# Preparing the second block's weights in the attention's last slots: transposed inputs, low parts on GpSimd, first products moved

## The chip, the cores and the metric

One core of a Trainium2 chip runs the whole kernel in one launch. The metric is device microseconds of one execution; lower is better. The engines are TensorE (PE, with its weight loads PEld), VectorE (DVE), ScalarE (ACT), GpSimd (POOL) and SyncE (SP), which issues nearly all DMAs. Each runs its own instruction list in order and waits on semaphores.

## The reference

Two decoder-like blocks on x of 16x64x512, with a context of the same shape. Only what the border between them touches is spelled out:

```python
# block 0: attention (32 query heads, 8 key/value heads of 128), then a quantised gated feed-forward
x = x + tanh(g_xattn[0]) * attention0(layernorm(x), ctx, mask, wq, wk, wv, wo)
x = x + tanh(g_ffn[0])   * quant_ffn(layernorm(x), Wg, Wu, Wd)
# block 1: q = Wq c + bq, k = Wk c + bk over 64 channels of the context, attention over the 512 positions
q = einsum('dc,bct->btd', Wq, init) + bq
k = einsum('dc,bct->bdt', Wk, init) + bk
out = softmax(q k) @ (einsum('oc,bct->bto', Wv, x) + bv)
# block 1: a base product and a low-rank part of 4 chosen experts out of 16, weighed by a router
y = einsum('bth,oh->bto', x, W_base) + b_base
z = einsum('bth,erh->bter', x, lora_A[active])
y += einsum('bteo,bte->bto', einsum('bter,eor->bteo', z, lora_B[active]) * 2, softmax(log(prior) + router(x)))
```

Products in full float32 are made of "hi" and "lo" parts: a ScalarE copy rounds a tensor to the hi part, a subtraction on another engine gives the lo part, and TensorE adds hi x hi, hi x lo and lo x hi.

## The kernel before

There are two programs, one after the other, without a barrier between them. The first, `attention_block`, does block 0's attention in 32 slots numbered U (0 to 31): 8 groups of key/value heads, two query-head pairs each, two halves of the tokens each. A slot of TensorE (`slot` under `@block.tensor`) holds in this order: the four output tiles of the unit before, `output(U - 1)` (six matmuls each, lines 521, 522, 526); four transposes of the probabilities (line 615); the scores of unit U + 1 (`score_unit`, line 503); the product with the values (line 628, "av"); then up to three projection items (lines 81 to 83). Slots 30 and 31 have no items left. What sets the order is the order written by hand in each engine's list, plus the semaphores.

The output tiles alternate between two PSUM banks, so tile k must wait until VectorE has added tile k - 2 into `x_res`: `output_tile` waits on `s_acc`, which `accumulate` (VectorE, line 927) raises, and which starts at 2:

```python
pe.wait_ge(s_acc, UT * U + tl + 1)
```

The other engines per slot: ScalarE copies the transposed probabilities (line 748), copies av to `oT_hi` (823), takes the exponential of the next unit (700), and evacuates projections (695, 696). VectorE adds four tiles (927), does the softmax of the next unit in `soft_first` (scale and mask 907, maximum 912, subtraction 914), makes `oT_lo` (1104), and sums the exponentials (921, 923). GpSimd multiplies by the inverse sum (1188), and rotates (1174, 1180) and splits (1151) the slot's projections.

The second program, `last_programs` (feed-forward of block 0 and block 1 interleaved by hand in `tensor`, `scalar`, `vector`, `gpsimd`, `sync`), needs prepared weights and the first tile of the context. This is the border, and it is made in slots 30 and 31 and just behind them:

- `load_block1` and `load_base` (SyncE) load the small weights and W_base. `lora_B` comes with 4 DMAs in runs of 8 floats.
- TensorE: `qkv_T` (533) transposes Wq, Wk, Wv; `base_T(0..3)` (545) transposes W_base, four 128x128 blocks each; `b_T` (561) transposes lora_B; `low_T` (552, 553, 556) picks the active experts' rows with selection matrices; `low_b_select` (567) does the same for lora_B; `first_qk` (576, 577) makes q and k of the first context tile. `qkv_T` and `base_T(0)` end slot 30; `base_T(1)` and `(2)` stand ahead of av in slot 31; `base_T(3)`, `b_T` behind it; then output tile 0 of unit 31, `first_qk`, `low_T((0, 1))`, tile 1, `x_transpose(0)` (1515), tile 2, `gate_mm(0, 0)` (1525) and so on, with `low_T((2, 3))` much later, behind `gate_mm(0, 2)`.
- ScalarE: `qkv_weights` (769, 772), `base_high_part` (776), `bT_copy` (780), `first_split_hi` (796), `first_hi_qk` (800), `low_part` (785 to 788).
- VectorE: `selection_of_experts` (from 1016), `selection_matrices` (to 1034), `gated_rows` (1061), `router_offset` (1055, 1057), `qk_w_low_part` (1040), `base_low_part` (1045), `first_lo_qk` (1050). In slot 31 also the statistics of tiles 0 to 3 (1072), and behind it `first_front` (1133), which quantises the first tile for the feed-forward; ScalarE ends that with line 1423.
- GpSimd: two iotas and two memsets at the head of slot 30 (1230 to 1233), raising `s_zero`; the low part of the first context tile (1246), the inverse deviation (1250), and four memsets (1255) for which SyncE waits before it starts its list of the second program.

```python
if U == 2 * NPAIR - 2:
    pool.iota(M.rank_i[:, :], pattern=[[1, RANK]], base=0, channel_multiplier=0).then_inc(s_zero, 1)
    pool.iota(M.part_i[:, :], pattern=[[0, 1]], base=0, channel_multiplier=1).then_inc(s_zero, 1)
    pool.memset(f32(M.qk_w_lo[:, :]), 0.0).then_inc(s_zero, 1)
    pool.memset(M.v_w[:, :], 0.0).then_inc(s_zero, 1)
```

## Time and profile before

| | us |
|---|---|
| three runs | 797.85, 799.20, 799.59; median 799.20 |
| the profiled execution | 797.15, of which its span is 795.3 |
| TensorE busy | 783.9 (99%), granted clock 1.00 |
| VectorE busy | 542.8 (68%) |
| ScalarE busy | 437.7 (55%) |
| GpSimd busy | 496.0 (62%) |
| TensorE busy between 563 and 582 | 18.0 of 19 |
| VectorE busy between 563 and 604 | 39.1 of 41 |

Times in the rows are microseconds from the span's start. A matmul's end is modelled and overlaps the next one's start, so on TensorE the distance from one start to the next is the cost of a piece of work. The attention's last slot but one (U = 30) starts on TensorE at 553.4, slot 31 at 563.6, and the second program's first gate product at 581.3.

### The profile page before, as it was taken

To read this page: it belongs to the slowest core of one execution; us is meant where nothing else is said; L and a number is where in the kernel's file an instruction comes from. 1 tells how busy PE (TensorE), PEld (TensorE's weight loads), DVE (VectorE), ACT (ScalarE), POOL (GpSimd) and SP (SyncE) were. 2 spreads that over 40 slices of the span, in tenths; PEclk is the share of its full clock that TensorE was granted. 3 is DMA by queue.
4 is the path that set the end of the run, shared out by engine and by line. 5 is a ranking of instruction groups with operands and counts; after the bars stand their busy time and mean duration, and the time that the engine had idled before them with its cause. 6 is when DMAs were issued, how large, how long until landed. Compare 5 with 4: busy or idle time off the path is not lost.

```text
span 795.3 us, 13637 instructions
## 1 busy us (share of the span) xinstructions
PE 783.9 (99%) x4977; PEld 643.0 (81%) x4994; DVE 542.8 (68%) x1043; ACT 437.7 (55%) x825; POOL 496.0 (62%) x429
## 2 busy tenths in 40 slices
PE   8999999999999999999999999999999999999998
PEld 8888888888888888788888888888765777777776
DVE  5867776566677545565665455465899997998874
ACT  4754445444444434443445343334579898888773
POOL 1697567645656764566666456645457885877753
PEclk9999999999999999999999999999999999999999
DMA  9411623523543131963213220167273413223101
GB/s 305 136 68 39 167 79 80 133 73 88 144 88 90 40 102 38 56 128 80 87 40 95 51 53 27 33 73 254 91 193 100 107 47 81 74 48 81 47 15 40
DMA packets 89986, 71.02 MB, mean 89 GB/s; under 512 B 53648, under 2 KB 69232, under 8 KB 89536
## 3 DMA queue, kind: packets, MB, share of 16 engines
q1 hardware_dynamic: 89248, 69.82, 35.8%
q8 instruction: 40, 0.66, 0.4%
q10 hardware_dynamic: 672, 0.33, 0.1%
q14 instruction: 26, 0.21, 0.1%
HBM read 49.04 MB, written 6.34 MB: 70 GB/s over the span
## 4 chain that ended last, share of the span: by engine, by line
PE 94%; DVE 3%; ACT 1%; DMA 1%; issue 0%; POOL 0%; SPq 0%; DVEq 0%
PE bank L81 12%; PE bank L83 12%; PE bank L82 12%; PE bank L526 7%; PE bank L521 7%; PE bank L522 7%; PE bank L503 7%; PE bank L628 4%; PE bank L1602 4%; PE bank L1588 3%; PE bank L1554 2%; PE bank L1525 2%; PE bank L1533 2%; PE bank L1578 2%; PE bank L615 2%; PE bank L1579 2%
## 5 line engine op out<-in xcount | busy, mean ns | idle before, releaser
L927 DVE SCALAR_TENSOR_TENSOR x_res<-bank,gate,x_res 128x512 f32<-128x512 f32 x128 | 95.4, 747 | 74.6 <-PE bank L526 74.2
L1188 POOL TENSOR_TENSOR prob<-prob,row_inv 128x512 f32<-128x512 f32 x32 | 33.5, 1046 | 168.5 <-DVE row_inv L923 168.5
L1174 POOL TENSOR_TENSOR rope_swap<-rope_swap,trig 128x512 f32<-128x512 f32 x80 | 103.6, 1296 | 34.2 <-ACT rope_swap L696 33.9
L695 ACT COPY rope_swap<-bank 64x512 f32<-64x512 f32 x80 | 46.7, 584 | 111.2 <-DVE rope_cos L898 108.7
L898 DVE TENSOR_TENSOR rope_cos<-bank,trig 128x512 f32<-128x512 f32 x80 | 54.2, 678 | 76.8 <-PE bank L83 74.4
L521 PE MATMUL bank<-wo_hi,oT_hi 128*128 128x512 f32 x256 | 101.8, 398 | 2.1 <-DVE x_res L927 1.5
L81 PE MATMUL bank<-xnT_hi,wq_hi 128*128 128x512 f32 x256 | 103.1, 403 | 0.0
L83 PE MATMUL bank<-xnT_hi,wq_lo 128*128 128x512 f32 x256 | 101.6, 397 | 0.0
L82 PE MATMUL bank<-xnT_lo,wq_hi 128*128 128x512 f32 x256 | 101.2, 396 | 0.0
L522 PE MATMUL bank<-wo_lo,oT_hi 128*128 128x512 f32 x256 | 100.9, 394 | 0.0
L1180 POOL TENSOR_TENSOR q_rope<-rope_cos,rope_swap 128x512 f32<-128x512 f32 x64 | 84.2, 1316 | 5.0
L526 PE MATMUL bank<-wo_hi,oT_lo 128*128 128x512 f32 x256 | 80.6, 396 | 0.3 <-DVE oT_lo L1104 0.2
L2946 POOL TENSOR_TENSOR b_e<-b_e,b_inv 128x512 f32<-128x512 f32 x64 | 68.3, 1081 | 18.9 <-DVE b_inv L2139 18.4
L748 ACT COPY probT<-bank 128x512 f32<-128x512 f32 x32 | 18.7, 585 | 101.9 <-PE bank L615 101.9
L823 ACT CAST oT_hi<-bank 128x512 fp32r<-128x512 f32 x64 | 34.4, 589 | 68.9 <-PE bank L628 68.9
L503 PE MATMUL bank<-k_rope,q_rope 128*128 128x64 f32 x512 | 61.0, 272 | 0.0
L521 PEld LDWEIGHTS bank<-wo_hi,oT_hi 128*128 128x128 f32 x256 | 48.2, 188 | 15.4 <-DVE x_res L927 2.5
L503 PEld LDWEIGHTS bank<-k_rope,q_rope 128*128 128x128 f32 x512 | 59.7, 192 | 0.5
L81 PEld LDWEIGHTS bank<-xnT_hi,wq_hi 128*128 128x128 f32 x256 | 48.1, 188 | 12.9
L526 PEld LDWEIGHTS bank<-wo_hi,oT_lo 128*128 128x128 f32 x256 | 48.0, 188 | 12.2 <-DVE oT_lo L1104 1.2
L83 PEld LDWEIGHTS bank<-xnT_hi,wq_lo 128*128 128x128 f32 x256 | 48.1, 188 | 11.3
L82 PEld LDWEIGHTS bank<-xnT_lo,wq_hi 128*128 128x128 f32 x256 | 48.1, 188 | 10.9
(257 smaller groups left out, 1943.9 us busy)
## 6 DMA issues: line engine op xcount, KB each, us to landing
wq_raw<-in_L_xattn_wq SPq DMA_DIRECT2D x16, 512.0 KB, 3.9
wo_raw<-in_L_xattn_wo SPq DMA_DIRECT2D x16, 512.0 KB, 3.9
xn<-in_L_ffn_Wd SPq DMA_DIRECT2D x16, 256.0 KB, 3.2
b_ctx<-in_ctx SPq DMA_DIRECT2D x32, 128.0 KB, 2.7
b_k_twice<-b_qk_hi SPq DMA_DIRECT2D x32, 128.0 KB, 2.4
w_T_dram<-w_out SPq DMA_DIRECT2D x28, 128.0 KB, 3.4
w_T<-w_T_dram SPq DMA_DIRECT2D x2, 1376.0 KB, 17.7
xn<-in_L_ffn_Wg SPq DMA_DIRECT2D x10, 256.0 KB, 3.3
```

What stands on the lines that cost most here:

```text
L81: pe.matmul(out, a_hi, b_hi, start=first, stop=False)
L82: pe.matmul(out, a_hi, b_lo, start=False, stop=False)
L83: return pe.matmul(out, a_lo, b_hi, start=False, stop=last)
L503: mm = pe.matmul(score[:, n * S:(n + 1) * S], q_rope[jp][:, b], k_rope[:, b * S:(b + 1) * S], start=True, stop=True)
L521: pe.matmul(out, oT_hi[:, tl, h], wo_hi[jp][:, h, :], start=(h == 0), stop=False)
L522: pe.matmul(out, oT_hi[:, tl, h], wo_lo[jp][:, h, :], start=False, stop=False)
L526: mm = pe.matmul(out, oT_lo[:, tl, h], wo_hi[jp][:, h, :], start=False, stop=(h == 1))
L898: dve.tensor_tensor(out=rope_cos[:, rp, :].rearrange("p (b s) -> p b s", s=S), in0=proj[stream % 2][:, :].rearrange("p (b s) -> p b s", s= ...
L927: dve.scalar_tensor_tensor(out=K.x[:, t, :], in0=wo_ps[t % 2][:, :], scalar=K.gate[:, 0:1], in1=K.x[:, t, :], op0=ALU.mult, op1=ALU.add).t ...
L1174: pool.tensor_tensor(out=sw, in0=sw, in1=sin_b, op=ALU.mult).then_inc(s_rope, 1)
L1180: pool.tensor_tensor(out=dst, in0=rope_cos[:, rp, :].rearrange("p (b s) -> p b s", s=S), in1=sw, op=ALU.add).then_inc(s_rope, 1)
L2946: pool.tensor_tensor(out=e[m % 4][:, :], in0=e[m % 4][:, :], in1=inv_total[:, n:n + 1].to_broadcast([P, D]), op=ALU.mult).then_inc(s_w, 1)
```

## The change

W_base, Wq and Wk, Wv, and lora_B are laid out on the host and loaded as they are used. That removes `qkv_T`, `base_T`, `b_T` and `bT_copy`. W_base's low parts are subtracted by GpSimd from SBUF. Several steps get another place. The memset of `v_w` is gone (its zeros are in the loaded tensor).

TensorE (the two waits that come first are in `low_T`: the one for 9 ahead of chunks 0 and 1, the one for 11 ahead of its last matmul; in the slot, the first pair of edits lies between the probability transposes and av, the second behind av; `x_transpose(0)` now waits for `s_w_low`):

```diff
+                pe.wait_ge(s_sel, 9)
+                pe.wait_ge(s_soft, 5 * (2 * NPAIR - 1) + 1)
...
+                pe.wait_ge(s_sel, 11)
...
             def first_qk(par):
                 if par == 0:
-                    pe.wait_ge(s_w_qkv, 4)
+                    pe.wait_ge(s_w_qkv, 1)
                     pe.wait_ge(s_w_qkv_lo, 1)
-                    pe.wait_ge(s_oT_lo, 2 * 2 * NPAIR)
+                    pe.wait_ge(s_proj_read, len(ALL))
...
                 if U == 2 * NPAIR - 1:
-                    base_T(1)
-                    base_T(2)
+                    low_T((0, 1))
...
                 if U == 2 * NPAIR - 2:
-                    qkv_T()
-                    base_T(0)
+                    first_qk(0)
+                    first_qk(1)
+                if U == 2 * NPAIR - 1:
+                    low_T((2, 3))
             run_slots(slot)
-            base_T(3)
-            b_T()
...
-            first.qk(0)
-            first.qk(1)
-            first.low_T((0, 1))
             first.output(2 * NPAIR - 1, 1)
             x_transpose(0)
...
             gate_mm(0, 2)
-            first.low_T((2, 3))
```

ScalarE (the first edit of the slot lies behind the copy of the transposed probabilities, the second behind `oT_hi`, the last two at the slot's end):

```diff
             def qkv_weights():
-                act.wait_ge(s_w_ps, W_QKV)
-                act.wait_ge(s_zero, 4)
...
+                act.wait_ge(R1.s_in, 16 * R1.n_loads)
+                act.wait_ge(s_zero, 3)
+                act.copy(M.qk_w_hi[:, :], R1.qk[:, :]).then_inc(s_w_qkv, 1)
+                act.copy(M.v_w[:, :], R1.v[:, :]).then_inc(s_w_qkv, 1)
...
                         probT_copy(U)
-                    if U == 2 * NPAIR - 1:
+                    if U == 2 * NPAIR - 2:
+                        first_split_hi(1)
                         base_high_part(1)
+                        base_high_part(2)
                     act.wait_ge(s_av, U + 1)
...
+                    if U == 2 * NPAIR - 2:
+                        first_hi_qk(0)
+                        first_hi_qk(1)
                     if U < 2 * NPAIR - 1:
                         exp_unit(U + 1)
...
+                    if U == 2 * NPAIR - 3:
+                        qkv_weights()
+                        first_split_hi(0)
+                        base_high_part(0)
                     if U == 2 * NPAIR - 2:
-                        qkv_weights()
-                        base_high_part(0)
-                        first_split_hi(0)
-                        first_split_hi(1)
+                        base_high_part(3)
                         prior_logarithm()
             run_groups(body)
-            base_high_part(2)
-            base_high_part(3)
-            bT_copy()
+            low_part()
```

VectorE (the first edit stands in the loop over the four tiles, behind `accumulate`):

```diff
                 for k in range(UT):
+                    if U == 2 * NPAIR - 2:
+                        (qk_w_low_part, selection_of_experts, selection_matrices, gated_rows)[k]()
                 if U == 2 * NPAIR - 2:
-                    selection_of_experts()
-                    selection_matrices()
-                if U < 2 * NPAIR - 1:
+                    soft_scale(U + 1)
+                    output_low(U)
+                    soft_shift(U + 1)
+                elif U < 2 * NPAIR - 1:
                     soft_first(U + 1)
+                    output_low(U)
                 else:
                     statistics_end()
-                    base_low_part(1)
-                    gated_rows()
                     router_offset()
+                    output_low(U)
                 if U < 2 * NPAIR - 1:
                     soft_sum(U + 1)
-                if U == 2 * NPAIR - 2:
-                    qk_w_low_part()
-                    base_low_part(0)
...
-            base_low_part(2)
...
-            first.base_low(3)
```

GpSimd:

```diff
                         pool.memset(f32(M.qk_w_lo[:, :]), 0.0).then_inc(s_zero, 1)
-                        pool.memset(M.v_w[:, :], 0.0).then_inc(s_zero, 1)
+                        first_split_lo(0)
+                        first_split_lo(1)
+                        pool.wait_ge(M.s_ctx_lo[1], 1)
+                        base_low_part(0)
+                        base_low_part(1)
                     if U < 2 * NPAIR - 1:
                         normalise(U + 1)
...
             run_groups(body)
-            pool.wait_ge(s_prob, 2 * NPAIR)
-            for par in range(2):
...
+            base_low_part(2)
+            base_low_part(3)
             pool.wait_ge(s_x_stat, 2 * UT + 1)
```

`first_split_lo` is the removed loop's body, `base_low_part` VectorE's old one with `R1.base` in SBUF in place of a PSUM bank. `qk_w_low_part` now waits for `s_w_qkv` at 1 (it was 4) and reads `R1.qk` in SBUF. `low_T` writes to the score bank, `first_qk` to the projection banks. SyncE issues one DMA for lora_B (4 before), and two for Wq, Wk and Wv (3 before).

## Rows read from the trace of the kernel before

**Rows 1.** The page: busy time of the engines.

```profile
PE 783.9 (99%) x4977; PEld 643.0 (81%) x4994; DVE 542.8 (68%) x1043; ACT 437.7 (55%) x825; POOL 496.0 (62%) x429
```

**Rows 2.** Windows: length, busy PE, PEld, DVE, ACT, POOL, granted clock, DMA share, GB/s.

```profile
563.00:573.00 10.00, 9.33 (x58) 6.99 (x56) 9.72 (x22) 8.08 (x17) 3.98 (x4) 1.00 0.01 2
...
592.00:604.00 12.00, 10.81 (x61) 6.65 (x60) 11.90 (x24) 10.74 (x24) 11.66 (x10) 1.00 0.41 110
```

**Rows 3.** The chain that ended last, 557 to 582: start, us, what.

```profile
557.60 0.23 PE bank L521
...
562.48 1.08 ACT oT_hi L823 x2
...
563.59 1.29 DVE oT_lo L1104 x2
564.88 0.60 DVE row_max L921
...
566.45 0.67 DVE x_res L927
...
575.94 0.24 PE bank L576
...
581.31 0.81 PE bank L1525 x3
```

**Rows 4.** Timeline of VectorE: start, us, line, [idle before].

```profile
554.86 0.75 DVE L927 SCALAR_TENSOR_TENSOR x_res<-bank,gate,x_res 128x512 f32<-128x512 f32 x1 [0.70 <-PE bank L526]
...
559.71 0.16 DVE L1016 CAST l_act_f<-l_act_i 128x4 f32<-128x4 int32 x1
...
562.11 0.69 DVE L912 TENSOR_REDUCE row_max<-prob 128x8 f32<-128x512 f32 x1
562.83 0.69 DVE L914 TENSOR_TENSOR prob<-prob,row_max 128x512 f32<-128x512 f32 x1
...
582.26 0.75 DVE L2070 SCALAR_TENSOR_TENSOR f_gate<-bank,f_x_scale,w_row 128x512 f32<-128x512 f32 x1 [0.55 <-PE bank L1525]
```

**Rows 5.** Timeline of GpSimd around the head of slot 30.

```profile
558.00 1.29 POOL L1180 TENSOR_TENSOR q_rope<-rope_cos,rope_swap 128x512 f32<-128x512 f32 x1
...
559.41 0.20 POOL L1232 MEMSET l_qk_lo<- 128x128 f32 x1
```

**Rows 6.** Timeline of ScalarE.

```profile
563.55 0.63 ACT L700 ACTIVATE prob<-prob 128x512 f32<-128x512 f32 x1
564.09 0.53 ACT L769 CAST l_qk_hi<-bank 64x128 fp32r<-64x128 f32 x2
...
578.32 0.72 ACT L1423 ACTIVATE f_xn<-f_xn,f_x_inv 128x512 f32<-128x512 f32 x1 [0.15 <-DVE f_x_inv L1417]
```

**Rows 7.** Timeline of TensorE: removed and moved pieces, and what follows each.

```profile
570.51 1.04 PE L545 MATMUL bank<-ident,l_raw_base 128*128 128x128 f32 x8
571.48 1.16 PE L628 MATMUL bank<-probT,v_nat 64*128 64x128 f32 x16
572.57 0.66 PE L545 MATMUL bank<-ident,l_raw_base 128*128 128x128 f32 x4
...
573.81 0.50 PE L521 MATMUL bank<-wo_hi,oT_hi 128*128 128x512 f32 x1
...
576.71 0.30 PE L552 MATMUL bank<-l_sel,l_raw_a 128*128 128x32 f32 x2
...
577.90 0.50 PE L521 MATMUL bank<-wo_hi,oT_hi 128*128 128x512 f32 x1
```

**Rows 8.** Waits of TensorE up to 560: total us, times, longest.

```profile
PE bank L521 <- DVE x_res L927: 1.5, 1, 1.5
```

**Rows 9.** Two timelines, VectorE and GpSimd, at the same moment.

```profile
587.83 0.68 DVE L2089 SCALAR_TENSOR_TENSOR f_h<-f_tanh,f_up 128x512 f32<-128x512 f32 x1
...
596.70 1.45 DVE L2089 SCALAR_TENSOR_TENSOR f_h<-f_tanh,f_up 128x352 f32<-128x352 f32 x1
...
596.50 1.27 POOL L2952 TENSOR_TENSOR b_ctx_split<-b_ctx,b_ctx_split 64x512 fp32r<-64x512 f32 x1
```

More of the change, by code:

```diff
@@ L554, in low_T @@
+                    pe.matmul(score[:, c * NLOW + NZ:(c + 1) * NLOW], R1.r[:, c * P:(c + 1) * P], M.sel_e[:, :], start=True, stop=True)
                 if cs[-1] < DC - 1:
                     return
-                pe.matmul(trans[:, HD:HD + E_ACT], M.spread[:, :], M.sel_e[:, :], start=True, stop=True).then_inc(s_w_lowT, 1)
-            def b_T():
-                pe.wait_ge(s_w_lo, 2)
-                for c in range(DC):
-                    mm = pe.transpose(proj[0][:, c * P:(c + 1) * P], R1.b[:, c, :], K.ident[:, :])
-                mm.then_inc(s_w_ps, 1)
+                pe.wait_ge(s_sel, 11)
@@ L633, in slot @@
                 if U == 2 * NPAIR - 2:
-                    qkv_T()
-                    base_T(0)
+                    first_qk(0)
+                    first_qk(1)
+                if U == 2 * NPAIR - 1:
+                    low_T((2, 3))
             run_slots(slot)
-            base_T(3)
-            b_T()
             output(2 * NPAIR - 1, (0,))
             first = Keep()
-            first.output, first.qk, first.low_T, first.low_b_select = output_tile, first_qk, low_T, low_b_select
+            first.output, first.low_b_select = output_tile, low_b_select
             tail.tensor(pe, first)
@@ L915, in soft_first, with output_low @@
                                   op=ALU.subtract).then_inc(s_soft, 1)
+            def soft_first(U):
+                soft_scale(U)
+                soft_shift(U)
+            def output_low(U):
+                dve.wait_ge(s_oT_hi, 2 * U + 2)
+                for par in range(2):
+                    dve.tensor_tensor(out=oT_lo[:, :, :, par, :],
+                                      in0=av[par][:, :].rearrange("p (t h q) -> p t h q", t=UT, h=2),
+                                      in1=f32(oT_hi[:, :, :, par, :]), op=ALU.subtract).then_inc(s_oT_lo, 1)
             def soft_sum(U):
@@ L1276, in block1_raw @@
     R, sb = Raw1(), area.take
-    R.qkv = [sb(f"l1_raw{i}", [S, S]) for i in range(3)]
+    R.qk, R.v = sb("l1_raw_qk", [P, P]), sb("l1_raw_v", [P, P])
     R.a = sb("l1_raw_a", [P, D])
-    R.b = sb("l1_raw_b", [P, DC, P])
+    R.b = sb("l1_raw_b", [P, D])
     R.r = sb("l1_raw_r", [E_ALL, D])
@@ L3264, in rope_table, with laid_out @@
     return np.ascontiguousarray(np.stack([cos, sin], axis=1).astype(np.float32))
+def laid_out(inputs):
+    a = {name: np.asarray(value) for name, value in inputs.items()}
+    base = a["L1_ffn_W_base"].T.reshape(DC, P, D).transpose(1, 0, 2)
+    qk = np.tile(np.concatenate([a["L1_xattn_Wq"].T, a["L1_xattn_Wk"].T], axis=1), (2, 1))
+    v_two = np.zeros((P, P), np.float32)
+    v_two[:S, :S] = v_two[S:, S:] = a["L1_xattn_Wv"].T
+    low_b = a["L1_ffn_lora_B"].transpose(0, 2, 1).reshape(P, D)
+    return [("base_T", base), ("qk_T", qk), ("v_T", v_two), ("lora_b_T", low_b),
+            ("rope_table", rope_table())]
 def kernel(**inputs):
@@ L3272 @@
     arrays, aps = {}, {}
-    for name, value in [*inputs.items(), ("rope_table", rope_table())]:
+    for name, value in [*inputs.items(), *laid_out(inputs)]:
         arrays["in_" + name] = v = np.ascontiguousarray(value)
```

124 lines of the change are left out of this document (40 added, 84 removed).

## The prediction

> **What bounds the kernel now.** The page comes first: TensorE is busy 99% of the span, its weight loads (81%) overlap it, and no other engine is over 68% [rows 1]. Over the whole kernel a microsecond taken from TensorE's list looks like a microsecond won. The windows around the border correct that. From 563 to 573 TensorE loses 0.7 us and VectorE is busy 9.72 of 10; from 592 to 604 TensorE loses 1.2 us and VectorE is busy 11.90 of 12 [rows 2]. So here VectorE sets the pace, and TensorE's transposes fill time in which it would partly wait. The chain says the same: it leaves TensorE at 562.46 (the end of av of unit 30), goes through ScalarE's `oT_hi`, VectorE's `oT_lo`, the sum of the exponentials and the addition of a tile, and stays on VectorE nearly until TensorE's 575.2 [rows 3]. The place ahead of it differs: at 557.60 TensorE is on the chain with the fourth tile of unit 29 [rows 3], and any wait put there is paid in full, because nothing ahead of 562.46 has slack on TensorE.
>
> **The change, first part: a new wait of VectorE in slot 30.** `qk_w_low_part` now stands behind the first of the four additions, and waits for ScalarE's copy, which waits for `s_zero` at 3, which GpSimd raises with the memset at the head of its slot 30. When is each there? The first addition starts at 554.86, and its result is there some 0.7 us later, at 555.55 [rows 4]. GpSimd works on its last rotation until 559.29 and ends the memset at 559.61 [rows 5]; the change takes nothing out of its list ahead of that. ScalarE's copy follows: two copies of 64x128 took 0.53, so one takes 0.27; the new one has 128 rows and reads SBUF; I bound it by 0.25 below and by the 0.63 of a 512-column ScalarE instruction above, and take 0.3, as the 64x128 copy is nearest [rows 6]: 559.92. The subtraction itself is of 64x128; 0.2 is an estimate from the 0.16 of a tiny instruction and the 0.69 of one of 512 columns [rows 4]. VectorE is free again at 560.12, having stood from 555.55 to 559.92.
>
> Queued behind it are the additions of tiles 1, 2, 3. TensorE's tile 3 needs the bank of tile 1, hence the second addition: 560.12 plus 0.67, as one such addition takes [rows 3], is 560.79, and TensorE starts the tile at 560.82. It did so at 557.60 [rows 3]. **That is +3.22 us**, and probabilities, scores and av follow in the same shape: av ends at 565.68, where it ended at 562.46. The selections that VectorE does in the same slot (they fill 559.71 to 562.11, together with the scaling of 0.7 [rows 4]), and its `gated_rows`, run while TensorE does the tile, transposes and scores; if they did not fit (say 1 us more), the scaling would be late, but `oT_lo` waits for av longer than that. I cost them at nothing. ScalarE's three copies ahead of `oT_hi` (0.6 each as the rows for 512 columns, [rows 6]) run before av ends; nothing again.
>
> **Second part: from av(30) to the third tile of unit 30.** Before: `oT_hi` and `oT_lo` end 2.42 behind av, and the addition of tile 0 ends at 567.12, that is 4.66 behind [rows 3]. After: VectorE does `oT_lo` first and then the maximum's reduction and the subtraction, 0.72 apart and 0.69 long [rows 4]; the exponential, 0.63, can only start then [rows 6]; then the sum, 0.60, the reciprocal, 0.2 with its start, and the addition, 0.67 [rows 3]. In all 2.42 + 0.72 + 0.69 + 0.63 + 0.60 + 0.2 + 0.67 = 5.93, with semaphore steps of 0.02 each about 6.0. TensorE has by then done `first_qk` and tiles 0 and 1 (at 4.6, as before) and waits for this addition: **+1.35 us**. What left VectorE here (`qk_w_low_part` and one base subtraction) is counted in the 4.66. What left TensorE (`qkv_T`, `base_T(0)`) lay where it waited for `oT_hi` anyway, and so does `first_qk` now.
>
> **Third part: slot 31 and the tiles of unit 31.** Eight transposes, 0.97, go from ahead of av(31), and `low_T((0, 1))`, 1.19, comes: +0.2. Behind av `base_T(3)` and `b_T`, 1.24, go, and `low_T((2, 3))`, 1.19 and one matmul more, comes; neither counts, as tile 0's last two matmuls wait for `oT_lo`, which follows from av. So tile 0 of unit 31 ends 1.35 + 0.2 = 1.55 later against av(30) than before: 13.48 then [rows 3], 15.0 now. Behind tile 0, `first_qk` (0.93) and `low_T((0, 1))` (1.19) go: −2.1 [rows 7]. But of this 2.1 only a part is won, as the next thing in TensorE's list waits for `x_transpose(0)`'s input. Before, tile 0 ended at 575.94, and ScalarE's last step of `first_front` at 579.04, 3.1 behind [rows 3, 6]; TensorE, with 3.5 us of work in between, didn't wait. Now there is one tile (1.4) in between, and TensorE waits 1.7. The quantised tile is there at 18.1, the transposes take 0.24, tile 2 takes 1.4 and a step 0.1, and the gate product starts at 19.85. Before it was 581.31, or 18.85 [rows 3]: **+1.0 us** in all, in place of the 1.55.
>
> **Fourth part: behind it.** VectorE waits 0.55 for the gate product at 582.26 [rows 4], so the base subtraction that leaves its list just ahead wins nothing. `low_T((2, 3))` leaves a stretch (589 to 591) of TensorE that ends in one bound by VectorE [rows 2]: worth nothing if VectorE never waits there, and 0.4 if the shorter of the two waits of [rows 2] (0.7 and 1.2) went by half; I take 0.2. GpSimd's and SyncE's lists start the second program some 1.2 us later against av(30), for GpSimd now has four base subtractions in between, some 1.3 each like its rotation [rows 5]; the duplicates of the first q and k then land just in time. The smaller loads on SyncE, far ahead, change nothing.
>
> One row is a warning for the upper end. A VectorE product of 352 columns took 1.45 us, where one of 512 took 0.68, while GpSimd ran a subtraction from 596.50 to 597.77 [rows 9]. The Trainium skill ("SBUF — State Buffer", Who interferes with whom) has it that a VectorE instruction with two SBUF inputs and a GpSimd one that reads SBUF exclude each other; this row agrees. Moving GpSimd's work deals such meetings anew; one costs up to 0.9 [rows 9].
>
> **Sum.** 3.22 + 1.0 − 0.2 = 4.0 us. The profiled execution took 797.15, so it would be 801.2; the median of three is 2 us above that execution, and on it the sum gives **803.2**.
>
> **The rivals.** *TensorE's list is all that counts (faster).* Removed are 0.97 and 1.24 [rows 7], and about 0.8 at the end of slot 30 (seven transposes, by the eight at 0.97), 3.0 in all: 796.2. It decides at one point: `s_w_qkv` must be raised before about 556.2, so that the second addition ends ahead of 557.6. It would need GpSimd to be 3.4 us earlier; GpSimd's records are rough, but ScalarE's and VectorE's around them are not. What speaks for it is the 99% [rows 1]. Chance 0.09.
>
> *The wait is there but the tail swallows it (no difference).* If the 0.7 and 1.2 us that TensorE loses in [rows 2], and its 3.0 us of transposes, could all be taken against the 3.2, little is left: 799.4. It needs the chain through `oT_lo` and the exponentials to be slack, which the chain shows it is not. Chance 0.10.
>
> *TensorE's clock falls over the new wait (still slower).* Its granted clock is 1.00 in every window of [rows 2], and over a wait of 1.5 us for the same addition [rows 8] nothing behind it took longer. A wait of 3.2 us no row shows. If the clock fell to the 1.2 GHz level, tile, transposes, scores and av behind it (from 557.60 to 562.46, 4.86 us) would at most double: up to 4.86 more, 808.1, and half of that 805.6. The Trainium skill ("TensorE: Matmul & The Clock Gate", What's actually happening) says that such a fall follows idleness. Chance 0.07.
>
> **The numbers.** Forecast 0.74, the three rivals 0.09, 0.10, 0.07. A run of this kernel can tell 0.2%, 1.6 us, from no change. The forecast's own range takes 0.2 off for `low_T`, 0.55 if VectorE's wait for the gate product [rows 4] is made good, adds 0.2 for `low_T`, 0.9 for one meeting, 0.3 for the copy, and the spread of the runs of before (1.4 below the median, 0.4 above): 801.0 to 805.0. To hold 8 in 10 it reaches to 800.0 below, towards the second rival, and to 805.6 above, past the lower price of the third. Faster 0.09, same 0.12, slower 0.79.
>
> **What would show it.** In the new profile VectorE's `qk_w_low_part` has an idle time of 4.4 us before it, released by ScalarE; TensorE waits some 3.2 us for the addition ahead of the last output tile of unit 29, and 1.3 ahead of the third of unit 30; `x_transpose(0)` waits over 1 us for ScalarE; the first gate product starts near 585.5. The forecast is wrong if VectorE's wait is under 1 us (then the first rival), or if the gate product is late but the wait of TensorE near 604 shrinks by as much.

## The result, and the profile after

The changed kernel takes 803.94 us, median of 10 runs (803.14 to 809.24), beside 798.34 for the kernel before on the same chip (10 runs, 797.11 to 802.37). The medians lie 5.6 us apart; the ratio is 1.008 with an interval of 1.0061 to 1.0098. The kernel is slower. The forecast was 803.2, with 800.0 to 805.6 as its range.

The page of the changed kernel, first the span and the engines (before: [rows 1]):

```profile
span 802.1 us, 13578 instructions
PE 782.9 (98%) x4954; PEld 641.2 (80%) x4971; DVE 542.7 (68%) x1039; ACT 437.0 (54%) x822; POOL 501.0 (62%) x432
```

The profiled execution took 803.9. TensorE is busy for 1.0 us less than before and needs 6.8 us more span, so what was added is mostly waiting. A part of the busy time is work at a lower clock, as shown below. The timeline of VectorE, around the head of slot 30, shows where:

```profile
555.23 0.75 DVE L911 SCALAR_TENSOR_TENSOR x_res<-bank,gate,x_res 128x512 f32<-128x512 f32 x1 [0.70 <-PE bank L523]
560.37 0.28 DVE L1024 TENSOR_TENSOR l_qk_lo<-l_raw_qk,l_qk_hi 64x128 fp32r<-64x128 f32 x1 [4.39 <-ACT l_qk_hi L739]
...
561.24 1.20 DVE L1000 CAST l_act_f<-l_act_i 128x4 f32<-128x4 int32 x1
...
564.94 1.31 DVE L1040 TENSOR_SCALAR l_base_row<-l_base_row,gate 128x512 f32<-128x512 f32 x1
566.17 1.24 DVE L1041 TENSOR_TENSOR l_bv<-l_bv,gate 128x1 f32<-128x1 f32 x1
```

The first addition (L911, line 927 of the kernel before) is followed by 4.39 us of nothing, released by ScalarE's copy. That copy, in ScalarE's timeline:

```profile
560.04 0.30 ACT L739 CAST l_qk_hi<-l_raw_qk 128x128 fp32r<-128x128 f32 x1 [4.30 <-POOL l_qk_lo L1214]
```

and what releases the copy, with what else GpSimd did, in GpSimd's timeline (compare [rows 5]):

```profile
559.75 0.20 POOL L1214 MEMSET l_qk_lo<- 128x128 f32 x1
561.14 1.27 POOL L1171 TENSOR_TENSOR b_ctx_split<-b_ctx,b_ctx_split 64x512 fp32r<-64x512 f32 x1 [1.19 <-ACT b_ctx_split L762]
564.70 1.27 POOL L1171 TENSOR_TENSOR b_ctx_split<-b_ctx,b_ctx_split 64x512 fp32r<-64x512 f32 x1 [2.29 <-ACT b_ctx_split L762]
566.04 2.60 POOL L1176 TENSOR_TENSOR l_base_lo<-l_raw_base,l_base_hi 128x512 fp32r<-128x512 f32 x2
```

It is a chain of three: memset, copy, subtraction, and behind the subtraction the second addition. In the kernel before, the tile that needs this addition started here:

```profile
557.44 0.40 PE L521 MATMUL bank<-wo_hi,oT_hi 128*128 128x512 f32 x1
```

TensorE's timeline of the changed kernel shows that tile's wait, and the waits that follow (L518 is line 521 of the kernel before):

```profile
561.37 0.50 PE L518 MATMUL bank<-wo_hi,oT_hi 128*128 128x512 f32 x1 [3.39 <-DVE x_res L911]
569.27 0.73 PE L523 MATMUL bank<-wo_hi,oT_lo 128*128 128x512 f32 x2 [0.59 <-DVE oT_lo L897]
572.83 0.50 PE L518 MATMUL bank<-wo_hi,oT_hi 128*128 128x512 f32 x1 [1.43 <-DVE x_res L911]
...
580.54 0.63 PE L519 MATMUL bank<-wo_lo,oT_hi 128*128 128x512 f32 x1
...
586.13 0.38 PE L1494 MATMUL bank<-ident_b,f_xn 128*128 128x128 bf16 x4 [1.56 <-ACT f_xn L1402]
588.03 0.38 PE L1504 MATMUL bank<-w_T,f_xqT 128*128 128x512 bf16 x1
610.95 0.22 PE L1525 MATMUL bank<-ident_b,f_h 128*128 128x128 bf16 x1 [0.84 <-ACT f_h L2522]
```

Forecast were waits of 3.2, 1.3 and 1.7; they are 3.39, 1.43 and 1.56. Not forecast are the 0.59, and the matmul of 0.63 us at 580.54, where such a one takes 0.39 elsewhere. The windows tell why (columns as in [rows 2]; the last but two is the granted clock):

```profile
578.00:580.00 2.00, 2.00 (x21) 1.76 (x17) 0.72 (x4) 1.07 (x2) 1.80 (x3) 1.00 0.00 0
580.00:582.00 2.00, 2.00 (x6) 1.61 (x6) 0.95 (x2) 0.73 (x3) 1.17 (x3) 0.50 0.00 0
582.00:584.00 2.00, 2.00 (x8) 1.57 (x7) 1.09 (x2) 0.00 (x0) 0.00 (x0) 0.65 0.57 146
```

At 580 the granted clock falls from 1.00 to 0.50 (from the 2.4 GHz level to the 1.2 GHz one), for some 3.4 us, in the middle of busy work and 7 us behind the last wait.

**How the runs below are compared.** Two profiles differ long before slot 30, in code that is the same: the first addition of slot 30 starts at 555.23 in one profile of the changed kernel and at 558.92 in the other. Near 340 us TensorE waits for an addition, 1.53 us before and 3.22 in the second profile of the changed kernel, and in that one the granted clock falls there too (as in those of `e3_gated_order` and `e7_memset`). So starts are counted from the first addition of slot 30. "The distance" is from there to the first gate product: 554.86 to 581.31 before, 26.45 us, and 26.34 in a second profile of the kernel before; 555.23 to 588.03 after, 32.80.

The columns give the starts on TensorE; the last one covers only the stretch from slot 30 to the gate product.

| kernel | probabilities of unit 30 | av(30) | probabilities of unit 31 | gate product | granted clock under 0.9 in |
|---|---|---|---|---|---|
| before | 3.98 | 6.41 | 15.21 | 26.45 | nowhere |
| before, second profile | 3.98 | 6.41 | 15.17 | 26.34 | nowhere |
| after | 7.65 | 9.91 | 20.49 | 32.80 | 580 to 584 |
| after, second profile (`a0`) | 8.33 | 11.51 | 21.61 | 32.79 | 566 to 570 |
| `e1_late` | 3.98 | 6.93 | 18.70 | 29.66 | nowhere |
| `e2_gated` | 8.88 | 11.29 | 21.39 | 32.35 | 562 to 566 |
| `e3_gated_order` | 8.43 | 11.50 | 19.90 | 32.32 | 562 to 568, 580 to 588 |
| `e4_all` | 3.98 | 6.92 | 17.90 | 30.00 | 578 to 582 |
| `e5_pool` | 3.98 | 6.91 | 16.90 | 29.32 | 576 to 580 |
| `b_wait` | 8.16 | 11.66 | 20.43 | 32.17 | 562 to 566 |
| `e7_memset` | 4.19 | 6.47 | 20.82 | 32.00 | 574 to 582 |
| `e8_memset_pool` | 4.19 | 6.47 | 17.98 | 30.08 | 570 to 574, 580 to 584 |
| `e6_own` | 3.97 | 6.44 | 14.86 | 25.69 | nowhere |

### The profile page after: what moved, and what is told of

It reads as the page before. It is cut to its first block, busy times and chain, and to the rows that moved or that the text cites. A ratio compares the mean times of both kernels' runs of the same rounds, so it can differ in the third digit from the quotient of the medians.

```text
span 802.1 us, 13578 instructions
## 1 busy us (share of the span) xinstructions
PE 782.9 (98%) x4954; PEld 641.2 (80%) x4971; DVE 542.7 (68%) x1039; ACT 437.0 (54%) x822; POOL 501.0 (62%) x432
## 4 chain that ended last, share of the span: by engine, by line
PE 92%; DVE 4%; POOL 2%; ACT 1%; issue 1%; DMA 1%; another core or an unknown queue 0%; SPq 0%; DVEq 0%; ACTq 0%
PE bank L81 12%; PE bank L83 11%; PE bank L82 11%; PE bank L523 7%; PE bank L518 7%; PE bank L519 7%; PE bank L500 7%; PE bank L600 4%; PE bank L1577 4%; PE bank L1563 3%; PE bank L1533 2%; PE bank L1504 2%; PE bank L1512 2%; PE bank L588 2%; PE bank L1555 2%; PE bank L1556 2%
## 5 line engine op out<-in xcount | busy, mean ns | idle before, releaser
L911 DVE SCALAR_TENSOR_TENSOR x_res<-bank,gate,x_res 128x512 f32<-128x512 f32 x128 | 95.4, 746 | 76.6 <-PE bank L523 74.9
L518 PE MATMUL bank<-wo_hi,oT_hi 128*128 128x512 f32 x256 | 102.5, 400 | 6.9 <-DVE x_res L911 5.0
L518 PEld LDWEIGHTS bank<-wo_hi,oT_hi 128*128 128x128 f32 x256 | 48.7, 190 | 21.1 <-DVE x_res L911 6.5
L519 PEld LDWEIGHTS bank<-wo_lo,oT_hi 128*128 128x128 f32 x256 | 48.6, 190 | 10.2
```

The costliest lines, as they stand in the source:

```text
L518: pe.matmul(out, oT_hi[:, tl, h], wo_hi[jp][:, h, :], start=(h == 0), stop=False)
L519: pe.matmul(out, oT_hi[:, tl, h], wo_lo[jp][:, h, :], start=False, stop=False)
L911: dve.scalar_tensor_tensor(out=K.x[:, t, :], in0=wo_ps[t % 2][:, :], scalar=K.gate[:, 0:1], in1=K.x[:, t, :], op0=ALU.mult, op1=ALU.add).t ...
```

## The experiments

The theory: VectorE's new wait in slot 30 costs 3.2 us, the order around `oT_lo` 1.35, and part of it comes back before the gate product. Rivals: only the rearranged weights matter, whatever the waits; or the clock makes the rest. The runs came in three batches, each with its own runs of the kernel before (medians 799.74, 797.97 and 802.12), so a median is compared inside its batch. The record also has a mean granted clock for each run, rounded to 0.001. It is 0.992 to 0.998 in the ten runs of the changed kernel. The kernel before has 1.000 in 13 of 28, 12 of 23 and 1 of 22 runs of the three batches: its clock falls too in some runs, and most often in the third.

**All four steps behind the fourth addition.**

```diff
-                    if U == 2 * NPAIR - 2:
-                        (qk_w_low_part, selection_of_experts, selection_matrices, gated_rows)[k]()
+                    if U == 2 * NPAIR - 2 and k == UT - 1:
+                        qk_w_low_part()
+                        selection_of_experts()
+                        selection_matrices()
+                        gated_rows()
```

> The changed kernel, with VectorE's four steps of slot 30 (qk_w_low_part, selections, gated_rows) behind its fourth addition in place of one behind each, so nothing of the additions queues behind the wait for s_w_qkv. My theory: the 3.4 us wait of TensorE ahead of the last tile of unit 29 goes, the 1.4 us one ahead of the third tile of unit 30 stays, and with less idling the granted clock stays at 1.00 near 580: about 4.5 us less than the changed kernel, some 799.5. Rival 1 (the wait costs but the clock falls all the same): about 3.2 us less. Rival 2 (the tail, not the wait, sets the time): under 1.5 us less.

Measured: 804.15 against 799.74, ratio 1.0053 (1.0028 to 1.0079); the distance is 29.66. The long wait is gone: the probabilities of unit 30 start 3.67 us earlier than in the first profile of the changed kernel. The distance is 3.14 shorter, and a part of that is the fall of the clock, which this one profile doesn't have. The median is not the 799.5 of the expectation: it is 4.4 above the kernel before, where the changed kernel stands 5.6 above it in its own batch, with intervals that overlap. So by time this run doesn't show what the wait costs. Eight of its ten runs have a mean clock of 0.998 or less. TensorE's waits in this kernel:

```profile
569.51 0.73 PE L523 MATMUL bank<-wo_hi,oT_lo 128*128 128x512 f32 x2 [1.58 <-DVE oT_lo L897]
573.07 0.50 PE L518 MATMUL bank<-wo_hi,oT_hi 128*128 128x512 f32 x1 [1.42 <-DVE x_res L911]
585.24 0.38 PE L1497 MATMUL bank<-ident_b,f_xn 128*128 128x128 bf16 x4 [1.85 <-ACT f_xn L1405]
```

A new one of 1.58 for `oT_lo` has come up: VectorE does the same small steps later, nearer to av, and several of them are stretched. Its timeline:

```profile
563.38 1.14 DVE L1008 TENSOR_SCALAR l_act_f<-l_act_neg 128x4 f32<-128x4 f32 x1
564.89 1.21 DVE L1018 TENSOR_SCALAR l_sel<-l_want,l_part_f 128x128 f32<-128x128 f32 x1
...
566.42 1.24 DVE L1041 TENSOR_TENSOR l_bv<-l_bv,gate 128x1 f32<-128x1 f32 x1
```

L1018 took 0.29 and L1041 0.15 in the changed kernel's second profile.

**The wait alone, in the kernel before.** Nothing of the change but two steps of the selections behind the first two additions.

```diff
-                if U == 2 * NPAIR - 2:
-                    selection_of_experts()
-                    selection_matrices()
+                    if U == 2 * NPAIR - 2 and k < 2:
+                        (selection_of_experts, selection_matrices)[k]()
```

> The kernel before, with selection_of_experts and selection_matrices behind the first and second addition of slot 30 in place of behind the fourth. The first waits for GpSimd's iotas at about 559.4. My theory: TensorE waits 3.2 to 3.5 us for the second addition, and the first gate product and all behind it come 3.2 to 3.5 us later, some 3.3 us more time. If the fall of the clock near 580 in the changed kernel was that wait's doing, it falls here too, and the distance to the gate product grows by up to 1.4 more. Rival: later slack takes most of the wait back, under 1.5 us.

Measured: 803.21 against 797.97, ratio 1.007 (1.0048 to 1.0092). VectorE waits behind its first addition, here for GpSimd's second iota:

```profile
559.39 0.20 DVE L1016 CAST l_act_f<-l_act_i 128x4 f32<-128x4 int32 x1 [3.93 <-POOL l_part_i L1230]
```

TensorE's timeline has the wait, with its restart, and the slow transposes and scores behind it:

```profile
561.00 0.50 PE L521 MATMUL bank<-wo_hi,oT_hi 128*128 128x512 f32 x1 [3.55 <-DVE x_res L927]
...
562.87 1.05 PE L615 MATMUL bank<-ident,prob 128*128 128x128 f32 x4
563.71 2.50 PE L503 MATMUL bank<-k_rope,q_rope 128*128 128x64 f32 x14
```

and its windows:

```profile
562.00:564.00 2.00, 2.00 (x9) 1.68 (x8) 0.89 (x2) 0.04 (x1) 0.00 (x0) 0.51 0.06 22
564.00:566.00 2.00, 2.00 (x14) 2.00 (x14) 0.00 (x0) 0.54 (x1) 0.00 (x0) 0.64 0.00 0
```

A wait at this one place makes 5.2 us by medians and 5.7 by the distance, nearly what the whole change makes, with all weights still transposed on TensorE. The rival of the rearranged weights falls. And behind the wait the clock comes down: from the last tile's start to av(30) there are 3.83 us before (557.44 to 561.27) and 5.37 here (561.00 to 566.37). So the wait costs 3.55 where it stands (the tile starts 3.71 later, counted from the first addition) and 1.5 more behind it. Another 0.5 is lost in the last stretch (11.74, before 11.24), where TensorE waits 0.69 for `oT_lo`.

The clocks of the single runs say the same. The four runs of `b_wait` have 0.997 to 0.998. The six runs of the kernel before with that clock have a median of 800.0, 3.2 us under `b_wait`; the twelve with 1.000 have 797.7. So of the 5.2 us some 3.2 are the wait and 2.0 go with the clock, an estimate from few runs.

**The changed kernel once more.**

> The changed kernel once more, on the chip of the next two. All theories: some 804 us, 5 to 6 above the kernel before on the same chip. It also shows where the granted clock falls in a second profile. If the fall belongs to the waits in slots 30 and 31, there is a window at 0.5 to 0.7 somewhere between 561 and 590, not necessarily at 580. If there is none and the time is the same, the clock is not part of the 5.6 us.

Measured: 809.22 against 802.12, ratio 1.0082 (1.0046 to 1.0118). Both kernels are slower on this chip, and both have lower mean clocks here (0.985 to 0.995 for the changed kernel). The difference of the medians, 7.1, has the widest interval of all. TensorE's timeline has the same wait:

```profile
565.07 0.50 PE L518 MATMUL bank<-wo_hi,oT_hi 128*128 128x512 f32 x1 [3.41 <-DVE x_res L911]
```

The windows have the fall directly behind the wait, and none at 580 or later:

```profile
566.00:568.00 2.00, 2.00 (x8) 1.60 (x7) 1.86 (x11) 0.00 (x0) 0.11 (x1) 0.50 0.37 144
568.00:570.00 2.00, 2.00 (x15) 2.00 (x14) 1.18 (x4) 1.65 (x4) 0.47 (x1) 0.71 0.00 0
...
580.00:582.00 2.00, 2.00 (x15) 1.72 (x14) 1.93 (x4) 0.58 (x1) 0.60 (x1) 1.00 0.00 0
```

So the clock falls at different places in two executions of one program, and in this stretch each pays once: from the last tile to av(30) 5.36 us here and 3.77 in the first profile; from the probabilities of unit 31 to the gate product 11.18 here and 12.31 there. The distances are 32.79 and 32.80.

**The gated rows back in slot 31, and the order of before besides.** `e2_gated` takes `gated_rows` out of the loop and puts it back into slot 31, behind `router_offset` (in the kernel before it stood just ahead of that). `e3_gated_order` also restores the order of the softmax and of the exponential:

```diff
-                        (qk_w_low_part, selection_of_experts, selection_matrices, gated_rows)[k]()
+                        (qk_w_low_part, selection_of_experts, selection_matrices)[k]()
...
                     soft_scale(U + 1)
-                    output_low(U)
                     soft_shift(U + 1)
+                    output_low(U)
...
-                        first_hi_qk(0)
-                        first_hi_qk(1)
                     if U < 2 * NPAIR - 1:
                         exp_unit(U + 1)
+                        first_hi_qk(0)
+                        first_hi_qk(1)
```

> The changed kernel, with gated_rows alone moved from slot 30 back to slot 31. There its two instructions took 1.31 and 1.24 us beside GpSimd's base subtractions, where one took 0.48 before. My theory: the collision made the scaling and so oT_lo 0.5 us late; without it 0.3 to 0.6 us less, the big wait and the fall of the clock stay. Rival: it was hidden, no change.

> As e2_gated, and the order of before in the softmax of unit 31: the maximum and its subtraction ahead of oT_lo on VectorE, the exponential ahead of the two q/k copies on ScalarE. My theory: TensorE's wait of 1.4 us ahead of the third tile of unit 30 goes; 1.6 us less than the changed kernel if the clock still falls near 580, 2.9 less if it does not. Rival: the next wait (for x_transpose) swallows it, under 0.5 us less.

Measured: 806.19 and 806.38 against 799.74, ratios 1.0076 (1.0049 to 1.0103) and 1.008 (1.0059 to 1.0101). `e2_gated` has a distance 0.45 shorter than the changed kernel, in its expected 0.3 to 0.6; but the second profile of the changed kernel has no long `gated_rows` either and still 32.79, so that this is the cause isn't shown. By time the order is worth nothing, which is the rival's number (under 0.5). The timelines of TensorE show that it does what it should. Without it:

```profile
562.50 0.80 PE L518 MATMUL bank<-wo_hi,oT_hi 128*128 128x512 f32 x1 [3.40 <-DVE x_res L911]
574.85 0.50 PE L518 MATMUL bank<-wo_hi,oT_hi 128*128 128x512 f32 x1 [1.43 <-DVE x_res L911]
587.02 0.38 PE L1495 MATMUL bank<-ident_b,f_xn 128*128 128x128 bf16 x4 [1.85 <-ACT f_xn L1403]
```

and with it:

```profile
562.99 0.50 PE L518 MATMUL bank<-wo_hi,oT_hi 128*128 128x512 f32 x1 [3.39 <-DVE x_res L911]
587.49 0.38 PE L1495 MATMUL bank<-ident_b,f_xn 128*128 128x128 bf16 x4 [0.69 <-ACT f_xn L1403]
```

The 1.43 is gone, and from av(30) to the probabilities of unit 31 there are 8.40 us in place of 10.10 (8.80 before): the order costs 1.3 to 1.7, the 1.35 of the forecast. Behind it the clock of this profile falls a second time:

```profile
580.00:582.00 2.00, 2.00 (x10) 1.83 (x10) 1.29 (x2) 1.25 (x5) 2.00 (x5) 0.65 0.00 0
582.00:584.00 2.00, 2.00 (x6) 1.55 (x5) 0.00 (x0) 0.14 (x3) 0.37 (x1) 0.50 0.16 40
```

and the last stretch takes 12.42 in place of 10.96, so that the distances, 32.32 and 32.35, are the same. All runs of the two kernels point the same way: their mean clocks have a median of 0.993 with the order and 0.997 without it. And one run of `e2_gated` has 1.000; it is its fastest, 803.99. So the long wait brings the clock down in all profiles here, but not in every run.

**Wait and order away together, then GpSimd's meetings too.** `e4_all` is `e3_gated_order` with the three remaining steps behind the fourth addition. `e5_pool` also moves GpSimd's first two base subtractions behind its normalisation of unit 31:

```diff
                         pool.wait_ge(M.s_ctx_lo[1], 1)
-                        base_low_part(0)
-                        base_low_part(1)
...
             run_groups(body)
+            base_low_part(0)
+            base_low_part(1)
             base_low_part(2)
```

> All of it: the three steps behind the fourth addition, gated_rows in slot 31, the softmax order of before. If the waits of VectorE and the order are the whole loss, the third tile of unit 30 starts near 568 in place of 572.8, and the time is 5 to 6.3 us below the changed kernel, 797.6 to 799, at or a little below the kernel before. Rival (moving the preparation itself costs, through GpSimd's base subtractions or ScalarE's copies ahead of the probabilities' copy): it stays 1.5 us or more above the kernel before.

> e4_all with GpSimd's base subtractions 0 and 1 behind the normalisation of unit 31 in place of ahead of it. In e4_all VectorE's subtraction of the maximum took 1.70 us in place of 0.69 beside one of them, and oT_lo followed it. My theory (the two engines exclude each other there): 0.69 again, TensorE's wait of 2.5 us for oT_lo shrinks to 1.5, and the distance from the first addition of slot 30 to the gate product falls from 30.0 to about 29.0, or less if the clock then stays up. Rival (the long record is an artefact or hidden): no change within 0.3.

Measured: 804.84 against 799.74, ratio 1.006 (1.0039 to 1.0081), distance 30.00; and 801.11 against 797.97, ratio 1.004 (1.0025 to 1.0055), distance 29.32 (one of its ten runs, 1557.26, stands far outside the others; its cause is not known). `e4_all` is no better than `e1_late`, and so its rival holds: 1.5 us or more stay above the kernel before. `e5_pool` comes out as expected on the wait, and somewhat longer in distance. VectorE's timeline in `e4_all`:

```profile
566.70 1.70 DVE L887 TENSOR_TENSOR prob<-prob,row_max 128x512 f32<-128x512 f32 x1
```

and in `e5_pool`:

```profile
565.92 0.69 DVE L887 TENSOR_TENSOR prob<-prob,row_max 128x512 f32<-128x512 f32 x1
```

The softmax's subtraction takes 1.70 beside GpSimd's base subtraction and 0.69 without it, and TensorE's wait for `oT_lo` goes from 2.48 to 1.48, the distance from 30.00 to 29.32. One meeting is worth 0.7 to 1.0 us here. `e5_pool` also has a fall of the clock, with nothing longer than that 1.48 ahead of it:

```profile
576.00:578.00 2.00, 2.00 (x10) 1.75 (x10) 1.29 (x2) 1.26 (x5) 1.81 (x4) 0.68 0.00 0
578.00:580.00 2.00, 2.00 (x6) 1.61 (x5) 0.08 (x1) 0.00 (x0) 0.00 (x0) 0.50 0.35 92
```

**The memset earlier.** The changed kernel, with the one instruction that heads the chain moved to the head of GpSimd's slot 29, where GpSimd stands idle for 6.4 us. The iotas stay (GpSimd waits for them ahead of its next subtraction).

```diff
+                    if U == 2 * NPAIR - 3:
+                        pool.memset(f32(M.qk_w_lo[:, :]), 0.0).then_inc(s_zero, 1)
                     if U == 2 * NPAIR - 2:
...
-                        pool.memset(f32(M.qk_w_lo[:, :]), 0.0).then_inc(s_zero, 1)
+                        pool.wait_ge(s_zero, 3)
                         first_split_lo(0)
...
-                act.wait_ge(s_zero, 3)
+                act.wait_ge(s_zero, 1)
...
-                dve.wait_ge(s_zero, 2)
+                dve.wait_ge(s_zero, 3)
```

> The changed kernel, with only the memset of qk_w_lo moved from the head of GpSimd's slot 30 to the head of its slot 29, where GpSimd stands idle. Theory (the memset releases ScalarE's copy, and this VectorE's subtraction, and so the second addition): ScalarE's copy runs near 555.9, TensorE's wait of 3.39 us ahead of the last tile of unit 29 is gone, and the distance from the first addition of slot 30 to the first gate product falls from 32.8 by 3.4 to 29.4, about like the run with all four steps behind the fourth addition; by medians 2.5 to 4 below the changed kernel on the same chip. The selections now wait for the iotas behind the second addition, so that oT_lo may be late by up to 1 us, 30.4. Rival (VectorE's own work in the slot, not the wait, is what costs): the distance stays within 1 us of 32.8.

Measured: 809.01 against 802.12, ratio 1.008 (1.0051 to 1.0109), and 809.22 for the changed kernel in the same batch. The distance is 32.00. The wait is gone and almost no time with it: the number is the rival's, and its mechanism (VectorE's own work in the slot) holds in part, as VectorE's steps take longer here, though because of GpSimd. VectorE's timeline:

```profile
563.40 1.11 DVE L1024 TENSOR_TENSOR l_qk_lo<-l_raw_qk,l_qk_hi 64x128 fp32r<-64x128 f32 x1
564.44 0.73 DVE L911 SCALAR_TENSOR_TENSOR x_res<-bank,gate,x_res 128x512 f32<-128x512 f32 x1
567.32 1.28 DVE L1000 CAST l_act_f<-l_act_i 128x4 f32<-128x4 int32 x1 [2.15 <-POOL l_part_i L1215]
...
568.76 1.08 DVE L1004 TENSOR_SCALAR l_act_neg<-l_act_f 128x4 f32<-128x4 f32 x1
...
570.07 1.15 DVE L1008 TENSOR_SCALAR l_act_f<-l_act_neg 128x4 f32<-128x4 f32 x1
571.14 0.74 DVE L911 SCALAR_TENSOR_TENSOR x_res<-bank,gate,x_res 128x512 f32<-128x512 f32 x1
```

The subtraction comes in time, and the step behind the second addition waits for the iotas, the next thing in GpSimd's list. Its instructions of four columns take 1.08 to 1.28 beside GpSimd's subtractions, the third addition comes at 571.14, and TensorE's timeline shows two later waits:

```profile
572.02 0.47 PE L518 MATMUL bank<-wo_hi,oT_hi 128*128 128x512 f32 x1 [0.71 <-DVE x_res L911]
...
575.84 1.22 PE L523 MATMUL bank<-wo_hi,oT_lo 128*128 128x512 f32 x2 [2.65 <-DVE oT_lo L897]
```

with a granted clock of 0.50 to 0.74 from 574 to 582. Up to av(30) all is as before (6.47, before 6.41); the whole loss stands between av(30) and the probabilities of unit 31, 14.35 us in place of 8.80. Of these 5.55 us the two waits are 3.4; the other 2.2 lie in a stretch in which the clock is down most of the time. VectorE is what is late here, and GpSimd what makes it late; an instruction moved alone only shows the next one.

**All terms undone but one.** `e8_memset_pool`: as `e7_memset`, with both selections behind the fourth addition, `gated_rows` in slot 31, the order of before, and GpSimd's two base subtractions late.

> As the run before, and besides: selections behind the fourth addition, gated_rows back in slot 31, softmax order of before, GpSimd's first two base subtractions behind the normalisation of unit 31. Every term of my sum but the last tile before x_transpose is undone. Sum by terms: no wait for the second addition, no collision ahead of oT_lo, no wait before the third tile of unit 30; what stays is x_transpose waiting for the quantised tile, 1 to 1.5 us. Distance 27 to 28 against 26.4 of the kernel before, and 798.5 to 800 on a chip on which the kernel before takes 798. Rival (the rearranged weights themselves, copies from SBUF in place of PSUM and GpSimd's subtractions, cost as well): over 29 and over 801. If the granted clock falls in this kernel too though it has no wait over 1 us in slot 30, the fall isn't tied to that wait.

Measured: 803.09 against 802.12, ratio 1.0017 (0.9997 to 1.0037): 6.1 below the changed kernel of the same batch, and not told apart from the kernel before. But its profile has a distance of 30.08, outside the 27 to 28 of the expectation and in the rival's range. The last wait that was to be gone is there, 1.65 for `oT_lo`, since two tiny selection steps took 0.99 and 1.10 beside GpSimd's split of the context; and the clock fell twice, at 570 and at 580, though no wait ahead of either fall is over 1.65 us. So a fall doesn't need the long wait. At the 0.9 to 1.6 us that a fall costs in the other profiles, two make 1.8 to 3.2 of this profile's 3.6 us, an estimate; and 21 of the 22 runs of the kernel before have a mean clock under 1.000 on this chip, so that the medians compare two kernels that both have falls. That would explain why they are so near. It isn't shown, as there is no profile of the kernel before on this chip, where its runs spread from 799.43 to 810.51.

**An order of its own, on the changed weights.** `e6_own` keeps the transposed inputs and GpSimd's low parts. VectorE has the selections behind the four additions, and `qk_w_low_part` and `gated_rows` in slot 31; the order of before; GpSimd's split of the context waits until the selections are done; TensorE has `first_qk` and the last of `low_T` behind tile 0 of unit 31, as before; ScalarE's copies follow these places:

```diff
                 if U == 2 * NPAIR - 1:
-                    low_T((0, 1))
+                    low_T((0,))
...
-                if U == 2 * NPAIR - 2:
-                    first_qk(0)
-                    first_qk(1)
                 if U == 2 * NPAIR - 1:
-                    low_T((2, 3))
+                    low_T((1, 2))
...
+                        pool.wait_ge(s_zero, 3)
+                        pool.wait_ge(s_sel, 9)
                         first_split_lo(0)
+                        pool.wait_ge(s_soft, 5 * (2 * NPAIR - 1) + 3)
                         first_split_lo(1)
...
+            first.qk(0)
+            first.qk(1)
+            first.low_T((3,))
             first.output(2 * NPAIR - 1, 1)
```

> An order of my own on the changed kernel's inputs: VectorE's selections and softmax as before, qk_w_low_part and gated_rows in slot 31; ScalarE makes the base's high parts while it is idle at the end of slot 29; GpSimd's subtractions only where VectorE has no instruction with two SBUF inputs; first_qk behind tile 0 as before; low_T in pieces where TensorE waits. My theory: every loss of the changed kernel is such a wait, so the distance to the gate product is 25.0 to 26.2, under the 26.45 of before, and the time 0 to 1.5 us under the kernel before. Rival (the transposed inputs, or the base parts on GpSimd, cost by themselves): over 1 us above the kernel before.

Measured: 797.72 against 797.97, ratio 0.9996 (0.9976 to 1.0015); the distance is 25.69, 0.76 under the kernel before. No fall of the clock. It is a tie: the distance and the time are inside the expectation, and the rival (the rearranged weights cost by themselves) fails. Its window of the stretch where [rows 2] had a busy TensorE of 9.33:

```profile
563.00:573.00 10.00, 8.44 (x52) 6.70 (x50) 9.66 (x23) 5.55 (x9) 8.05 (x8) 1.00 0.02 9
```

TensorE is busy 8.44 of 10 us, VectorE 9.66 (9.72 before): removed transposes have turned into waiting.

A second profile of the kernel before was taken in the second batch.

> The kernel before once more, for a second profile of it beside the next three. Measured from VectorE's first addition in slot 30 to the first gate product it took 26.45 us in its first profile, and 49.4 to the transposes of the first quantised h. Both theories expect the same distances within 0.2 us; what differs between executions should lie ahead of slot 30, in the slots after 336 us, where the profiles so far differ by up to 2 us for no edit.

Measured: 796.66 us in one run, with a distance of 26.34; the two profiles of the kernel before agree within 0.11 on it, and those of the changed kernel within 0.01.

## Why the prediction was right, and where a size was off

The sign, the place and the chain hold. By steps, from the table's columns (after less before):

| step | forecast | first profile | second profile |
|---|---|---|---|
| up to av(30) | +3.22 | +3.50 | +5.10 |
| av(30) to the probabilities of unit 31 | +1.35 | +1.78 | +1.30 |
| from there to the gate product | −0.35 | +1.07 | −0.06 |
| gate product to the transposes of the first hidden tile | −0.2 | 0.00 | −0.01 |
| sum | 4.0 | 6.35 | 6.33 |

- **The new wait** was forecast with 4.4 on VectorE and 3.22 on TensorE; they are 4.39 and 3.39. Counted from the first addition, the tile starts 3.56 later than before. The forecast had its start of before from the chain's row, 557.60; the timeline has 557.44, and this reading is 0.16 of the 0.34 that is missing. The subtraction took 0.28, not 0.2, and the addition behind it 0.74, not 0.67. `e1_late` and `b_wait` take the wait away and make it: at the probabilities of unit 30, 3.67 us less and 4.18 more (the latter with the clock already down).
- **The order around `oT_lo`**: 1.35 forecast, 1.30 in the second profile. The first has 0.48 more than that, and a wait of 0.59 for `oT_lo` that the second doesn't have. VectorE's `gated_rows`, which I had costed at nothing, took 1.31 and 1.24 for its two instructions beside GpSimd's subtractions, in place of 0.48 and 0.15 in the second profile. The caution of the forecast, that one meeting costs up to 0.9, is about the right size (1.0 for the subtraction of `e4_all`); that it strikes instructions of one and four columns too, I hadn't seen. `e4_all` and `e5_pool` show it for an instruction with two inputs in SBUF: taking GpSimd's subtraction away brings 1.70 back to 0.69. The rule of the Trainium skill named in the prediction ("SBUF — State Buffer", Who interferes with whom), which is about a VectorE instruction with two SBUF inputs, agrees with that. The cast of 1.20 (L1000) and the step of 1.14 in `e1_late` (L1008) read only one tensor, so two inputs aren't needed for such a meeting.
- **The gate product**: where no clock fell, the last stretch took 11.18, 10.96 and 10.96 (`a0`, `e1_late`, `e2_gated`) against 11.24 before. 0.06 to 0.28 came back, less than the 0.35. `x_transpose` waits 1.56 to 1.85, forecast 1.7.
- **Behind it** nothing comes back or is lost: from the gate product to the next transposes 22.92 us before, 22.92 after. The 0.2 for `low_T((2, 3))` was nothing, and so the second rival (the tail swallows the wait) fails.
- **The mis-sized term is the clock.** I made the fall a rival of chance 0.07 and put nothing for it in the sum. It is part of the likeliest case: each of the five profiles with a wait of 3.39 us or more shows one. It costs 1.4 to 1.6 right behind the wait (5.14 to 5.37 from the last tile to av(30) in `e2_gated`, `e3_gated_order`, `a0` and `b_wait`, against 3.77 in the first profile), or 0.9 to 1.5 later (12.10 to 12.42 in the last stretch where a fall lies in it, against 10.96 to 11.18 in changed kernels without one). With 1.5 for it the sum is 5.5, beside 5.6 by medians and 6.3 by the distance. The rival's lower price, half of 4.86, was still too high.
- **Why the number was good all the same**: by luck in part. I added 4.0 to a median of 799.20, while the kernel before had 798.34 beside the changed one. The 0.9 too much there makes up for half of the 1.6 that the sum lacked; 803.2 is nearer than its sum is.
- The first rival (TensorE's list counts) fails on every run: each kernel with the changed weights has 23 matmuls fewer (4954 in place of 4977 in the two first profiles), and none is faster than the kernel before beyond its interval.

## What to carry to other kernels

Before a small step is put into another engine's gap, follow its semaphore to the end: who raises it, and what that engine has ahead of it. A tiny memset at the wrong place in GpSimd's list made TensorE wait 3.4 us through three engines, and it did so because the additions that free the banks were queued behind the waiter. Moving it alone won almost nothing (32.80 to 32.00), as the next item of the same list did the same harm. Fill the gaps of the engine that does not set the pace only after the one that does has been freed (here VectorE, and GpSimd against it), and add to a long TensorE wait what its clock loses afterwards.

## What the runs showed of the hardware

- The granted clock fell to 0.50 in every profile with a TensorE wait of 3.39 us or more at this place, but at different times: at once in `b_wait`, `e2_gated`, `e3_gated_order` and `a0`, and 18.6 us behind its end in the first profile of the changed kernel, in the middle of work that kept TensorE busy for 2.00 of 2 us. It fell also in `e4_all`, `e5_pool` and `e8_memset_pool`, whose longest waits ahead of the fall are 2.48, 1.48 and 1.65, and not in the profile of `e1_late`, with 1.58 and 1.42 there. The Trainium skill ("TensorE: Matmul & The Clock Gate", What's actually happening) ties the fall to idleness; the falls right behind the long wait agree, and these others no single wait explains. What sets the moment stays open.
- One fall lasts some 3.4 to 7 us here and costs 0.9 to 1.6 us; in `e3_gated_order` the wait for `x_transpose` shrinks from 1.85 to 0.69 behind it and hides a part.
- Executions differ in it without any edit: in the second batch the kernel before takes 796.91 to 798.18 us in its twelve runs with a mean granted clock of 1.000, and 798.76 to 802.75 in its seven runs with 0.998 or less.
- A VectorE instruction of four or of one column beside a GpSimd subtraction of 512 columns took 1.0 to 1.3 us in place of 0.15 to 0.17 wherever it was stretched (L1000, L1004, L1008, L1041). Small doesn't mean cheap there.
